# Square FFN layers as seven block products instead of eight, weights streamed through a ring, on one Trainium2 core

## The reference

```python
xn = _layernorm(x)
x = x + attn(xn) + ffn(xn)          # attn: linear attention, 16 heads of 16, proj, layernorm, residual

def ffn(x):                          # _tlin(x, w, s) = einsum('bsi,oi->bso', x, w) * s; w holds -1, 0, 1
    h = silu(_tlin(x, w1_w, w1_s)) * _tlin(x, w2_w, w2_s)      # 256 -> 1024
    h = gelu(_tlin(h, h1_w, h1_s), approximate=False)          # 1024 -> 1024
    h = gelu(_tlin(h, h2_w, h2_s), approximate=False)          # 1024 -> 1024
    return _tlin(h, w3_w, w3_s)                                # 1024 -> 256
```

## Time and profile before

| | us |
|---|---|
| median of 3 runs (lowest, highest) | 1606.19 (1605.28, 1607.11) |
| span of the profiled execution | 1605.2 |
| TensorE busy in it | 1591.0 |
| VectorE busy | 945.4 |
| ScalarE busy | 527.6 |
| GpSimd busy | 38.1 |

### The profile page before, as it was taken

How to read it: one execution, slowest core, us unless ns; L and a number is a source line. 1 busy time by engine, 2 the same in 40 slices (tenths; PEclk the granted TensorE clock), 3 DMA queues, 4 the chain that set the end, 5 groups by cost and what they waited for, 6 DMA issues and landing times.

```text
span 1605.2 us, 22443 instructions
## 1 busy us (share of the span) xinstructions
PE 1591.0 (99%) x7884; PEld 1326.0 (83%) x7884; DVE 945.4 (59%) x1927; ACT 527.6 (33%) x817; POOL 38.1 (2%) x44
## 2 busy tenths in 40 slices
PE   8999999999999999999999999999999999999998
PEld 5888888888888888888888888888888888888886
DVE  5656657466564656647566474664746646566563
ACT  3324142241423424233242332423324143241421
POOL 1000000000000000000000000000000000000000
PEclk9999999999999999999999999999999999999999
DMA  9000000000000000000000000000000000000000
GB/s 355 23 12 11 27 18 22 11 11 27 18 22 18 4 27 18 22 22 0 27 18 27 18 9 18 18 27 18 18 9 18 27 18 22 11 11 27 18 10 20
DMA packets 28114, 42.07 MB, mean 26 GB/s; under 512 B 2112, under 2 KB 26816, under 8 KB 27328
## 3 DMA queue, kind: packets, MB, share of 16 engines
q1 hardware_dynamic: 26800, 29.12, 5.7%
q0 software_dynamic: 864, 11.53, 1.8%
q10 hardware_dynamic: 432, 1.18, 0.2%
HBM read 33.44 MB, written 8.39 MB: 26 GB/s over the span
## 4 chain that ended last, share of the span: by engine, by line
PE 99%; DMA 0%; DVE 0%; POOL 0%; issue 0%; DVEq 0%; POOLq 0%
PE ps L386 74%; PE ps L519 7%; PE ps L391 4%; PE ps L392 4%; PE ps L393 4%; PE ps L442 2%; PE ps L431 2%; PE ps L452 1%; PE ps L401 1%; DMA x<-in_H 0%; DVE wqkv_parts L850 0%; DVE xn L714 0%; DVE bn_stats L708 0%; POOL rstd L353 0%; DVE xn L837 0%
## 5 line engine op out<-in xcount | busy, mean ns | idle before, releaser
L386 PE MATMUL ps<-hidden_a,w_ffn 128*128 128x512 f32 x2048 | 488.1, 397 | 0.0
L386 PE MATMUL ps<-hidden_b,w_ffn 128*128 128x512 f32 x2048 | 484.4, 396 | 0.0
L386 PEld LDWEIGHTS ps<-hidden_b,w_ffn 128*128 128x128 f32 x2048 | 383.5, 188 | 91.6
L386 PEld LDWEIGHTS ps<-hidden_a,w_ffn 128*128 128x128 f32 x2048 | 381.4, 188 | 88.5
L622 ACT ACTIVATE value_ring<-ps,vectors 128x512 f32<-128x512 f32 x256 | 173.1, 689 | 693.7 <-PE ps L386 684.4
L386 PE MATMUL ps<-xnT,w_ffn 128*128 128x512 f32 x1024 | 249.4, 398 | 0.0
L386 PEld LDWEIGHTS ps<-xnT,w_ffn 128*128 128x128 f32 x1024 | 190.1, 188 | 43.6
L803 DVE CAST hidden_a<-value_ring 128x512 fp32r<-128x512 f32 x128 | 54.5, 426 | 216.0 <-ACT value_ring L622 216.0
L789 DVE SCALAR_TENSOR_TENSOR value_ring<-ps,vectors,gate_ring 128x512 f32<-128x512 f32 x128 | 94.2, 746 | 83.5 <-ACT gate_ring L604 83.5
L519 PEld LDWEIGHTS ps<-w_ffn,hidden_a 128*128 128x128 f32 x1024 | 123.9, 188 | 2.9
L519 PE MATMUL ps<-w_ffn,hidden_a 128*128 128x256 f32 x1024 | 124.6, 279 | 0.0
(11 more groups left out here) (76 smaller groups left out, 1338.8 us busy)
## 6 DMA issues: line engine op xcount, KB each, us to landing
raw_weights<-in_w_ffn SPq DMA_DIRECT2D x64, 176.0 KB, 2.3
w_ffn<-in_w_ffn POOLq DMA_DIRECT2D x5, 2048.0 KB, 14.0
x<-in_H SPq DMA_DIRECT2D x16, 512.0 KB, 3.6
out_dram<-acc SPq DMA_DIRECT2D x32, 256.0 KB, 2.2
w_ffn<-in_w_ffn POOLq DMA_DIRECT2D x1, 1024.0 KB, 24.6
wqkv_raw<-in_w_attn ACTq DMA_DIRECT2D x1, 768.0 KB, 5.5
row_vectors<-in_rows SPq DMA_DIRECT2D x1, 512.0 KB, 7.8
wproj_raw<-in_w_attn ACTq DMA_DIRECT2D x1, 256.0 KB, 6.8
```

The source lines that it names most:

```text
L386: r = mm(bank, a, b, start=first and part == 0, stop=last and part == 1)
```

## The change

The product of a 1024x1024 weight matrix A and the activations B of a tile is cut into quarters: A11 to A22 of 512x512, and B11 to B22, where the first index halves the features and the second the tokens. Instead of eight products of quarters seven are formed (Strassen's scheme in Winograd's form), from four raw and four combined operands on the side of B (`X_OF`: T1 = B12 - B11, T2 = B22 - T1, T3 = B22 - B12, T4 = B21 - T2) and three raw and four summed ones on the side of A.

A square layer is done in two passes, each for two of the four 128-row chunks of either half of the outputs, so a tile has passes 0 to 3. A pass is seven products, a product 16 matmuls of 256 columns (2 output chunks, 4 input chunks, 2 parts). Products are summed in PSUM where the scheme allows (three banks), and otherwise VectorE adds a bank to a kept partial sum in SBUF (`sum_into`); ScalarE keeps the first product (`keep_first`). The differences T1 to T4 are made on GpSimd (`t1` to `t4`), two of them on VectorE; high parts of all operands are copied by ScalarE; low parts are made by VectorE and GpSimd, as the lists `DVE_LO` (21 names) and `POOL_LO` (15 names) say; `POOL_T` holds 14 differences, `DVE_T` two.

The weights of the square layers no longer stay in SBUF. A ring of seven slots (512 KB each) holds the seven weight blocks of one pass; when a product is done, GpSimd issues the DMA that fills its slot for the next pass (`refill`), 28 a tile, from the input or from `weight_sums` in DRAM. The sums are made once: SyncE loads four raw blocks of each of four sets, VectorE makes the sums of sets 0 and 3, GpSimd those of sets 2 and 1, GpSimd stores them. Sets 2 and 3 are staged where gated values of tile 0 will stand. The gate and output weights stay resident. The check of low bits has five pieces a tile, two of them of the sums. In the prologue the split of the projection's weights stands ahead of `residual`. In `body` the output group of the second half comes first. Tile 0 is written out on its own, ahead of the loop.

The core of the diff (`gated`, `normalise`, the layer norms and attention keep their work):

```diff
+HK = HC // 2
+HT = N // 2
+BLOCK_COLS = HK * 2 * P
+SETS = 4
+A11, A12, A21, A22 = range(4)
+PRODUCTS = 7
+X_OF = {1: "B11", 2: "B21", 3: "B22", 4: "T4", 5: "T1", 6: "T2", 7: "T3"}
+RAW_OF = {1: A11, 2: A12, 4: A22}
+SUM_OF = {6: 0, 3: 1, 7: 2, 5: 3}
+ORDER = ((1, 5, 6, 7, 2, 4, 3), (1, 6, 2, 5, 7, 3, 4), (1, 5, 6, 2, 7, 4, 3), (1, 6, 2, 5, 7, 3, 4))
+BANKS = ((0, 1, 4), (5, 2, 3), (0, 1, 4), (5, 2, 3))
+ADDS = (("u", "w", "C22", "C21", "C12"), ("u", "v", "C22", "C12", "C21")) * 2
+GELUS = (("C11", "C22", "C21", "C12"), ("C11", "C22", "C12", "C21")) * 2
+OUT_BANKS = (4, 0)
...
+    def product_bank_read(t, s, i):
+        if s % 2 == 0:
+            own = {2: (first_kept.sem, first_kept.at(t, s)), 7: add.after(t, f"{s}u"), 4: add.after(t, f"{s}w"),
+                   3: add.after(t, f"{s}C22")}
+        else:
+            own = {2: (first_kept.sem, first_kept.at(t, s)), 5: add.after(t, f"{s}u"), 3: add.after(t, f"{s}v"),
+                   4: add.after(t, f"{s}C22")}
+        if i in own:
+            return own[i]
+        gated = lambda o: (h_made.sem, h_made.at(t, o))
+        return {(0, 1): gated(6), (0, 6): gated(6), (0, 5): gated(5),
+                (1, 1): gated(5), (1, 6): gated(7), (1, 7): gated(7),
+                (2, 1): gelu.after(t, "0C11"), (2, 6): add.after(t, "0C21"), (2, 5): add.after(t, "0C12"),
+                (3, 1): gelu.after(t, "1C11"), (3, 6): add.after(t, "1C12"), (3, 7): add.after(t, "1C21")}[s, i]
...
+            def load_set(i):
+                for b in range(4):
+                    sp.dma_start(stage[i][:, b], hidden_block(i, b)).then_inc(s_set[i], 16)
...
+                sp.wait_ge(s_wproj, 2)
+                load_set(0)
+                load_set(2)
+                load_set(3)
+                for i in (5, 6, 7, 3):
+                    sp.wait_ge(ring_loaded[i].sem, ring_loaded[i].at(t, 0))
+                sp.wait_ge(s_stored[0], 16)
+                load_set(1)
...
+            def weight_sums(i):
+                pool.wait_ge(s_set[i], 64)
+                a11, a12, a21, a22 = (stage[i][:, b] for b in range(4))
+                tt(a22, a21, a22, ALU.add).then_inc(s_sums[i], 1)
+                tt(a21, a11, a21, ALU.subtract).then_inc(s_sums[i], 1)
...
+            def store_sums(i):
+                pool.wait_ge(s_sums[i], 4)
+                dst = sums_dram[4 * i:4 * i + 4].rearrange("b p (j o) -> p b j o", j=HK)
+                pool.dma_start(dst, stage[i][:]).then_inc(s_stored[i], 16)
...
+            def refill(t, s, i):
+                pool.wait_ge(*prod.after(t, f"{s}P{i}"))
+                pool.sem_inc(refill_begun.sem, 1)
+                pool.dma_start(ring[:, i - 1], product_weights((s + 1) % SETS, i)).then_inc(ring_loaded[i].sem, 16)
...
+                    staging = isinstance(t, int) and t == 0
+                    t1(t, "G0")
+                    if staging:
+                        weight_sums(1)
+                        store_sums(1)
+                    t1(t, "G1")
+                    t2(t, "G0")
+                    t3(t, "G0")
+                    t4(t, "G0")
+                    t2(t, "G1")
+                    t3(t, "G1")
+                    lo(t, "G0", "T3")
+                    t4(t, "G1")
+                    lo(t, "G0", "B21")
+                    lo(t, "G0", "T4")
+                    lo(t, "G0", "B22")
+                    if staging:
+                        pool.wait_ge(s_stored[1], 16)
+                    if filling:
+                        refill(t, 0, 1)
+                        refill(t, 0, 6)
+                    lo(t, "H0", "B11")
+                    if filling:
+                        refill(t, 0, 5)
+                        refill(t, 0, 7)
+                        refill(t, 0, 2)
+                    t1(t, "H0")
+                    t3(t, "H0")
+                    t2(t, "H0")
+                    if filling:
+                        refill(t, 0, 3)
+                        refill(t, 0, 4)
+                    inverse_root(t, ln2_var, ln2_rstd)
+                    lo(t, "H0", "T1")
+                    lo(t, "H0", "T2")
+                    if staging:
+                        pool.wait_ge(s_stored[2], 16)
+                    if filling:
+                        refill(t, 1, 1)
+                        refill(t, 1, 6)
+                        refill(t, 1, 2)
+                    t4(t, "H0")
+                    if filling:
+                        refill(t, 1, 5)
+                    lo(t, "H0", "T3")
+                    lo(t, "H0", "B21")
+                    if filling:
+                        refill(t, 1, 7)
+                    lo(t, "H0", "T4")
+                    lo(t, "H0", "B22")
+                    t3(t, "H1")
+                    if filling:
+                        refill(t, 1, 3)
+                        refill(t, 1, 4)
+                    t4(t, "H1")
+                    lo(t, "H1", "B21")
+                    if more:
+                        ln1(t + 1)
+                    lo(t, "H1", "T3")
+                    lo(t, "H1", "T4")
+                    pool.wait_ge(*difference_made(t, "H1", "T2"))
+                    lo(t, "H1", "B22")
+                    if staging:
+                        pool.wait_ge(s_stored[3], 16)
+                    if filling:
+                        refill(t, 2, 1)
+                        refill(t, 2, 6)
+                        refill(t, 2, 5)
+                        refill(t, 2, 2)
+                        refill(t, 2, 7)
+                        refill(t, 2, 4)
+                        refill(t, 2, 3)
...
+                pool.wait_ge(s_qkv_raw, 16)
+                pool.dma_start(w[:, 0:W_OUT], w_ffn[:, 0:F_HID]).then_inc(s_w_gate, 16)
                 ln1(t)
-                for i in range(1, len(w_pieces)):
-                    load_weights(i)
-
-            over_tiles(pool, 0, prologue, body)
-            second_pass_if_needed(pool, lambda: over_tiles(pool, B, ln1, body))
+                for i in RAW_OF:
+                    pool.dma_start(ring[:, i - 1], product_weights(0, i)).then_inc(ring_loaded[i].sem, 16)
+                weight_sums(2)
+                store_sums(2)
+                store_sums(0)
+                for i in (5, 6, 7, 3):
+                    pool.dma_start(ring[:, i - 1], stage[0][:, SUM_OF[i]]).then_inc(ring_loaded[i].sem, 16)
+                store_sums(3)
+                pool.dma_start(w[:, W_OUT:], w_ffn[:, F_OUT:]).then_inc(s_w_out, 16)
...
+                def product(t, s, i):
+                    block_of_b = X_OF[i]
+                    groups = ("G0", "G1") if s < 2 else ("H0", "H1")
+                    firsts = (1, 6, 5) if s % 2 == 0 else (1, 6, 7)
+                    lasts = (2, 4, 3)
+                    bank = product_bank(s, i)
+                    pe.wait_ge(*product_bank_read(t, s, i))
+                    loaded = (exact_loaded if full else ring_loaded)[i]
+                    pe.wait_ge(loaded.sem, loaded.at(t, s))
+                    for m in range(2):
+                        for g, group in enumerate(groups):
+                            buf, slot = operands(group)
+                            for part in range(2):
+                                if m == 0 and s % 2 == 0:
+                                    if part == 0:
+                                        pe.wait_ge(*hi_made(t, group, block_of_b))
+                                    else:
+                                        pe.wait_ge(*lo_made(t, group, block_of_b))
+                                for j in range(2):
+                                    begins = m == 0 and g == 0 and part == 0 and j == 0
+                                    ends = m == 1 and g == 1 and part == 1 and j == 1
+                                    r = mm(bank[:, m * HT:(m + 1) * HT],
+                                           ring_weights[:, i - 1, 2 * g + j, m * P:(m + 1) * P],
+                                           as_used(buf[:, j, slot[block_of_b], part, :]),
+                                           start=i in firsts and begins, stop=i in lasts and ends,
+                                           skip_group_check=True)
+                    r.then_inc(prod.sem, 1)
...
+                hi_of_difference(t, "H0", "T1")
+                keep_first(t, 1)
+                hi_of_difference(t, "H0", "T3")
+                hi_of_difference(t, "H0", "T2")
+                gelu_of(t, 1, "C11")
+                hi_of_block(t, "H1", "B11")
+                hi_of_difference(t, "H0", "T4")
+                gelu_of(t, 1, "C22")
+                hi_of_block(t, "H1", "B22")
+                gelu_of(t, 1, "C12")
+                hi_of_difference(t, "H1", "T1")
+                gelu_of(t, 1, "C21")
+                keep_first(t, 2)
+                hi_of_difference(t, "H1", "T2")
+                hi_of_block(t, "H1", "B21")
+                hi_of_difference(t, "H1", "T3")
+                hi_of_difference(t, "H1", "T4")
...
+            def sum_into(t, s, i, dst, kept):
```

(29 more changed lines are left out.)

755 lines of the change are left out of this document (519 added, 236 removed).

## The result

| | before | predicted | after |
|---|---|---|---|
| median, us | 1606.61 (1605.28 to 1607.11) | 1568 | 1854.77 (1853.32 to 1856.27) |
| ratio to before | 1 | 0.976 | 1.155, 95% interval 1.1537 to 1.1564 |
| span of the profiled execution | 1605.2 | | 1851.5 |
| first product of a square layer, tile 0 | 45.5 | 89 | 106.3 |
| a tile in mid-run | 98.77 | 93 | 110.42 |

(A tile in mid-run is the distance from the first square product of tile 1 to that of tile 14, divided by 13.) The prediction was wrong in sign. Sixteen tiles at 110.42 instead of 98.77 are +186.4 us, the later start is +60.8; together 247 of the 246 us by which the span grew. Predicted were -86 and +48: the miss of some 285 us is nearly all in the steady tile.

The account below looks back on a forecast made before the run. TensorE's summed matmul spacings were taken as the bound. 1605.2 - 117.7 (fewer matmuls) + 48 (first tile) + 32 (steady-tile stalls) = 1567.5, so 1568 us; own range 1545 to 1600, 8 in 10 from 1525 to 1650.

Parts of the forecast that it names:

- Columns decide a matmul's cost: Square layers on TensorE: 256-column matmuls cost 0.1169 us against 0.2333 for 512 columns, a gain of 117.7 us.
- Totals: Busy time per tile: VectorE about 66 us, ScalarE about 55, GpSimd 50; none reaches TensorE's 91.
- The price of GpSimd: A 128x512 operation on GpSimd was taken at 1.1 us, bounds 0.69 and 1.6; a refill's issue at 0.57.
- the deciding point of 1.28: GpSimd's price per operation from which stalls reach 4.4 us a tile and the gain is used up.
- the end of 2.3: Upper bound in us for issuing a refill of 512 short runs on GpSimd, four times 0.57.
- the queue of 20.5 us: GpSimd's steady-tile queue, t1 of H0 to low part B21 of H1: 13 operations, 9 refills, one root.
- this rival: GpSimd's queue becomes the bound, TensorE waiting on its low parts in pass 2: 1630 to 1680 us, chance 0.20.
- ln2_apply and add_v: Pass 1 of a steady tile: ln2_apply ends at 44.3, add_v at 45.0; product 3 waits 0.6 us.
- the rule: Rival: VectorE operations with two SBUF inputs and GpSimd operations reading SBUF exclude each other; 1627 to 1687 us, chance 0.13.
- Small stalls: Steady-tile waits: 0.8 and 0.2 us for GpSimd's low parts in pass 2, 0.4 for slot 1 in pass 3.
- The start: First tile: making weight sums delays product 1 from 45.5 to about 89; 45 us plus 3 for low clock.

Follow-up runs that it names:

- the last run: Changed kernel with all fifteen of GpSimd's low parts left out and memsets of zero written in their place: 1654.31 us, ratio 1.0295.

## Why the prediction was wrong, point by point

- **Columns decide a matmul's cost: right.** 0.1183 us in a clean stretch against 0.1169 assumed. 7168 of them make 848 us, so the gain of 117.7 was 107.6; this miss is 10 us.
- **Totals: right in kind, wrong in use.** VectorE was forecast at 66 busy of 91 us a tile. Busy in all are 1334 us, 83 a tile. Of the 17 too many 14 are time held up: (204.5 - 128 x 0.48) / 16 = 8.9 in `ln2_apply`, (65.7 - 64 x 0.41) / 16 = 2.5 in `ln1_apply`, 208 x 0.22 / 16 = 2.9 in low parts. GpSimd was forecast at 50 and is at 59 in the tile from 862.08. No total reached the period, and still the tile grew by 11.7 us.
- **The price of GpSimd: 1.1 us taken, 1.25 to 1.29 measured** (1291 ns for L563's form, which meets little of VectorE). It lies within the bounds and just at the deciding point of 1.28. The refill's issue was 0.57 taken, 0.55 (128 runs) and 0.76 (512 runs) measured, so the end of 2.3 was far off. With both, the queue of 20.5 us would be 13 x 1.29 + 9 x 0.64 + 1.07 = 23.6. Yet the waits that this rival foresaw, TensorE's for GpSimd's parts in pass 2, cost 0.7 us a tile: TensorE had already lost 9 us in pass 1, and the parts were nearly ready. That the first hides the second is an argument; no run separates them.
- **ln2_apply and add_v: the step that failed.** The prediction had the inverse root end at 40.8 of a tile and `ln2_apply` take eight times 0.42 (its own row reads 0.481), so that `add_v` costs 0.6 us. In the tile from 862.08 the root ends 44.0 us in and `ln2_apply` takes 12.9 us: 8.99 of wait, then 2.6 of low clock. In all this is 11.6 of the 17.4 us by which the tile missed its forecast. The root's 3.2 us of delay are not in the wait, since TensorE itself comes to product 3 at 48.6 instead of 44.4; the 9.1 us that `ln2_apply` takes over its 3.8 are. The prediction named the rule and gave it 0.13 at 1627 to 1687; it spread the loss evenly over a stretch, as 3.7 to 7.5 us of work, and never asked which instruction stands under GpSimd's densest run of reads and what is queued behind it. It was also priced one for one, which is what the run without refills shows (1.52 us at most); with a refill issued in between, a VectorE operation can lose more than one GpSimd operation (4.75 us in one of 0.48).
- **Small stalls: the low parts right, the refills in the wrong place and low.** The low parts B21 and T3 of H1 were forecast at 0.8 and 0.2 (by its own terms the first is 55.8 less 55.1, 0.7) and cost 0.7 together (11.5 us in 31 waits). Refilled slots were forecast at 0.4, in pass 3 on slot 1, and cost 1.4 (22.2 us in 19 waits), nearly all of it in pass 1 on slot 2, whose refill stands behind those of slots 5 and 7 in GpSimd's queue. A refill also lands in 5 to 6 us and not in 3.3. That came from a 512 KB load by SyncE on nearly idle queues; here GpSimd's queue carries 246 MB.
- **A stall not seen:** the transposes wait 1.7 us a tile (30.0 in all, 4.9 of it in the prologue) for `ln1_apply`, which takes 1085 ns in place of 408.
- **The start: order right, sizes low.** 48 forecast with bounds 41 to 58, measured 60.8, just outside them. The sums cost 2.33 us each, within the bounds. The steps that were short are transfers: set 1 could be summed at 90 instead of 75, since the four ring blocks took 13.9 us beside the stores and set 1 had to wait for them.
- **The rest.** 9.1 + 2.6 + 1.7 + 1.4 + 0.7 + 0.6 (spacing) = 16.1 of the 19.0 us between the tile of 110.42 and the bare 98.77 - 7.36 = 91.41. The other 2.9 are not assigned to single causes.

**The rule against this case.** The Trainium skill, "SBUF — State Buffer", section "Who interferes with whom", says that such a pair excludes each other for the whole instruction, that a GpSimd instruction which only writes doesn't, and that `tensor_scalar` can contend too, through a two-port mode. On the first two the trace agrees: 2163 and 1147 ns against 481, and 480 beside memsets. How long such a wait can get is told by the runs alone: 1.52 us without refills, up to 4.95 with them. On the third it shows that the form is held up (1085 against 408 ns), and in the last run beside memsets too (1.53 us); whether it ran in that mode no row here tells. Its "GPSIMD Engine Reference", section "Performance versus the Vector engine", has 1.96 times VectorE's time, which would be 1.36 us, an estimate; measured is 1.29 against 0.69, 1.87 times.

## What to carry to other kernels

Before work is put on GpSimd, list VectorE's operations that read two SBUF inputs (and its `tensor_scalar`s from SBUF), mark those that run in the same stretch, and price them at their own time plus all of GpSimd's reads beside them, and DMA issues between the reads; then follow what is queued behind them, since a wait of 9 us for one sum stopped TensorE while VectorE as a whole was busy for only 72% of the span. Beside VectorE's work out of PSUM GpSimd cost nothing here (681 ns). Its memsets cost `ln2_apply` nothing but held up a `tensor_scalar`, and its DMA issues alone cost nothing in most places and 1 us in nine. A scheme that saves an eighth of the matmuls must also find a place for its one-time sums: here 60 us of start cost more than the 13 that the shorter tile gives with most collisions gone.
